# Two attention blocks and a feed-forward over 16 sequences: the feed-forward's first weights and first norm prepared inside the last attention phase

## The chip, the core and the metric

One core of one Trainium2 chip runs the whole kernel. The metric is the time of one execution on the device, in microseconds (us). Engines: TensorE (PE, with its weight loads as PEld), VectorE (DVE), ScalarE (ACT), GpSimd (POOL) and SyncE (SP), which issues all the DMAs.

## What is computed

16 sequences of 256 tokens and 512 channels go through a layer with quantised attention, a gated feed-forward and a last attention:

```python
h1 = _ln(x, ln1_g, ln1_b)
x = _attn(h1, h1, a1_wq, a1_wk, a1_wv, a1_wo, a1_bo, d_q1, d_k1, d_v1, d_w1) + x
h2 = _ln(x, ln2_g, ln2_b)
x = _attn(h2, context, a2_wq, a2_wk, a2_wv, a2_wo, a2_bo, d_q2, d_k2, d_v2, d_w2) + x
h3 = _ln(x, ln3_g, ln3_b)
hg = h3 @ ff_w1 + ff_b1
a, g = jnp.split(hg, 2, axis=-1)
x = a * jax.nn.gelu(g, approximate=False) @ ff_w2 + ff_b2 + x
```

Then comes `_L1_xattn_ref`: 8-head attention with queries from this x and keys and values from the context, both normed. `_attn` rounds q, k, v and the probabilities to 8 bits. All matrices are 512 wide; the feed-forward is 512 to 4096 to 512.

## The kernel before, in words

**Attention part (first block of engine programs).** The work is a row of 32 phases, each one attention of one sequence, in 8 slots (groups) of two heads. In slot g the engines do, for the phase at hand: PE the scores of two groups ahead (`pe_scores`, odd slots only, both groups at once) and the probabilities times values of an earlier pair (`pe_pv`); DVE the row maxima (`dve_max`) and the scaling of the probabilities (`dve_probs`); POOL two tiny products, `pool_bias` and `pool_dsum`; ACT the exponentials (`act_exp`, four per group); SP the DMA transpose of the probabilities from `pq` to `pT` (`turn_probs`), which waits for the probabilities and for the P·V that frees its buffer. Into the slots are laid "fills", the projections for neighbouring phases, by hand-written tables such as `P_Y_FILLS`: `("k2", 0)` is the first half of the keys of attention 2, `o1` and `o2` the output projections, `h2T` the turning of the normed x on PE. Fills write the two PSUM banks `PJ` in turn; `act_quantise` (or `dve_residual`) empties them. The context is cast into a high and a low part (`ctxT`) in slots set by `ctx_at`: ACT in slot `ctx_at - 1`, DVE in `ctx_at`, POOL in `ctx_at + 1` (`pool_long`, ahead of POOL's other work of the slot).

All engines run in order, so every wait holds back what stands behind it. The last two phases are P_Y (attention 1 of the last sequence, with the fills for its attention 2) and P_Z (that attention 2). Behind P_Z come a drain (`pe_drain`: P·V of groups 4 to 7), the last output projection `o2@15`, its residual and its store to `mid_dram`; then all engines meet at a barrier.

**Feed-forward part (second block).** It is done in two halves of the hidden width. Each half holds 8 chunks f of the weights (256 columns of `ff_w1`, 128 rows of `ff_w2`) and passes over all 16 sequences ("rounds" below, `pe_sequence_a` in the first half). For a sequence PE does 8 times `pe_up` (24 matmuls into bank AG of f mod 2) and, two chunks behind, `pe_down` (6 matmuls into Y); between them the chunk's gate (ACT), product and cast (DVE) and low part (POOL); then the projections k and v of the context for the last attention. In round 0 of the first half the weights are made on the way: SP loads a chunk in three DMAs into one of two staging buffers, ACT casts it to the high part (`act_weights_high`), DVE subtracts to get the low part (`dve_weights_low`), and PE waits for `w_low_done`. Before that round the block needs the first sequence back from `mid_dram`, its norm on DVE and POOL (`ln_stats`, `ln_rstd`, `ln_xhat`), its turning on PE and its high and low parts (`h3_parts`). SP's order there: sequence 0, chunk 0, context, two rows, chunk 1, two pieces of `w2` (the weights Wk, Wv), chunk 2, then a wait for `base_ready`, sequence 1, store of `h3T`, chunk 3, and so on. `base` is sequence plus bias, made by POOL (`pool_base`, line 1870) behind the first `pool_mid_low`.

## Time and profile before

| | us |
|---|---|
| median of 3 runs | 2743.24 |
| lowest and highest run | 2740.99 to 2746.74 |
| the profiled execution, its own time | 2741.51 |
| its span in the trace | 2739.7 |
| barrier at the end of the attention part | 1062.58 |
| first AG matmul of the feed-forward | 1075.17 |

The page lists 54077 instructions; PE is busy 2575.7 us (94%), DVE 1642.4 (60%), ACT 1420.1 (52%), POOL 678.6 (25%). In its 40 slices of 68.5 us the digits of PE are 9 nearly everywhere but for the first two slices and the 15th and 16th, 6 and 4 (959 to 1096 us), where the granted clock also stands at 7 tenths. Times in the trace are counted from the start of the span; a line such as `L701` is a line of the kernel before.

### The profile page before, as it was taken

The page shows a single profiled execution, that of the slowest core. Times are in us where ns is not written, and L with a number is a line of the kernel's source. Part 1 is how long each engine was busy: PE and PEld are TensorE (multiplying, and loading weights), DVE is VectorE, ACT ScalarE, POOL GpSimd, SP SyncE. Part 2 cuts the span into 40 slices and gives each one's busy share as a digit, 9 for nine tenths or more (in the row PEclk, how much of TensorE's full clock was granted, in tenths as well). Part 3 has the DMA queues.
Part 4 walks back from the last instruction along what each step waited for, and adds up shares of the span by engine and source line. Part 5 has one row for each costly group of instructions (what it writes and reads, how often), then busy time and mean ns, then how long its engine had stood idle before and what let it go on. Part 6 is the DMA issues. An engine that isn't in the chain of part 4 may idle for free.

```text
span 2739.7 us, 54077 instructions
## 1 busy us (share of the span) xinstructions
PE 2575.7 (94%) x18304; PEld 2151.3 (79%) x18304; DVE 1642.4 (60%) x3945; ACT 1420.1 (52%) x3749; POOL 678.6 (25%) x1147
## 2 busy tenths in 40 slices
PE   5799999999999964999999999999999999999997
PEld 4566676676667642899999999999888888888885
DVE  6799999999999964634444443454443444444444
ACT  5688888888888862211112111123555555555554
POOL 1222222222222211323222222322221222222211
PEclk9899999999999977999999999999999999999998
DMA  4444444444444535311121211141111111111111
GB/s 151 94 95 100 93 98 97 100 92 96 99 93 96 93 63 144 105 69 69 54 84 54 77 56 74 61 150 66 47 54 38 54 54 46 46 46 54 46 38 39
DMA packets 335273, 211.06 MB, mean 77 GB/s; under 512 B 275568, under 2 KB 291952, under 8 KB 335216
## 3 DMA queue, kind: packets, MB, share of 16 engines
q1 hardware_dynamic: 335216, 210.34, 28.8%
q8 instruction: 31, 0.51, 0.1%
q14 instruction: 26, 0.21, 0.0%
HBM read 92.84 MB, written 50.33 MB: 52 GB/s over the span
## 4 chain that ended last, share of the span: by engine, by line
PE 56%; DVE 2%; issue 1%; ACT 1%; DMA 0%; POOL 0%; DVEq 0%; SPq 0%; POOLq 0%
PE AG L156 35%; PE Y L156 13%; PE XT L1314 3%; PE O L1337 2%; PE XT L1324 2%; PE XT L131 1%; DVE parts L1658 1%; DVE xhat L123 1%; PE Y L131 1%; PE O L1347 0%; DVE turned L185 0%; ACT stage L1554 0%; DMA stage<-in_ff_w_dram 0%; DVE mid_parts L1715 0%; POOL base L1870 0%
## 5 line engine op out<-in xcount | busy, mean ns | idle before, releaser
L156 PE MATMUL AG<-h_parts,up 128*128 128x256 f32 x6144 | 778.6, 284 | 13.4 <-DVE down L1639 10.1
L156 PEld LDWEIGHTS AG<-h_parts,up 128*128 128x128 f32 x6144 | 762.6, 192 | 26.0 <-issue 10.9
L599 ACT ACTIVATE e<-S,bias,qk_scale 128x256 f32<-128x256 f32 x1024 | 562.9, 569 | 113.5 <-POOL bias L805 113.5
L1522 ACT ACTIVATE gate<-AG,cols_pack 128x256 f32<-128x256 f32 x256 | 121.6, 475 | 668.8 <-PE AG L156 668.3
L1885 POOL TENSOR_TENSOR mid_parts<-mid_act,mid_parts 128x256 fp32r<-128x256 f32 x256 | 199.9, 781 | 1078.9 <-DVE mid_parts L1715 1078.9
L156 PE MATMUL Y<-down,mid_parts 128*128 128x512 f32 x1536 | 403.6, 399 | 0.0
L1708 DVE SCALAR_TENSOR_TENSOR mid_act<-AG,cols_pack,gate 128x256 f32<-128x256 f32 x256 | 123.4, 482 | 422.9 <-ACT gate L1522 421.9
L701 DVE TENSOR_REDUCE negmax<-S 128x4 f32<-128x1024 f32 x256 | 302.5, 1218 | 60.5 <-PE S L499 60.5
L156 PEld LDWEIGHTS Y<-down,mid_parts 128*128 128x128 f32 x1536 | 271.9, 189 | 68.7 <-issue 22.6
L719 DVE TENSOR_SCALAR pq<-e,rsum 128x256 uint16<-128x256 f32 x1024 | 292.1, 348 | 15.7 <-DMA pT<-pq 3.0
L147 PE MATMUL PJ<-w_a_wo,oT 128*128 128x512 f32 x512 | 239.4, 612 | 3.6 <-ACT oT L608 2.7
L156 PE MATMUL PJ<-hT,w_a_wq 128*128 128x256 f32 x1536 | 205.9, 292 | 29.9 <-DVE hT L690 24.5
L156 PEld LDWEIGHTS PJ<-hT,w_a_wq 128*128 128x128 f32 x1536 | 193.7, 197 | 46.0 <-issue 29.5
L599 ACT ACTIVATION_READ_ACCUMULATOR e<-S,bias,qk_scale 128x1 f32 x1024 | 212.7, 208 | 0.0
L156 PEld LDWEIGHTS AG<-parts,w_late 128*128 128x128 f32 x1536 | 190.5, 191 | 4.5 <-issue 0.6
L156 PE MATMUL AG<-parts,w_late 128*128 128x256 f32 x1536 | 192.0, 283 | 0.0
L147 PEld LDWEIGHTS PJ<-w_a_wo,oT 128*128 128x128 f32 x512 | 95.1, 195 | 109.1 <-issue 109.1
L567 ACT ACTIVATE q<-PJ,inv 128x512 int8<-128x512 f32 x192 | 130.6, 701 | 91.1 <-PE PJ L156 91.1
L1744 DVE TENSOR_REDUCE negmax<-XT 128x2 f32<-128x512 f32 x128 | 82.5, 686 | 104.9 <-PE XT L1314 104.9
L1715 DVE CAST mid_parts<-mid_act 128x256 fp32r<-128x256 f32 x256 | 84.4, 330 | 86.5 <-PE Y L156 82.1
L1554 ACT ACTIVATE stage<-XT,negmax 128x256 f32<-128x256 f32 x256 | 118.1, 473 | 29.0 <-DVE negmax L1744 28.5
L1522 ACT ACT_TABLE_LOAD x59 | 75.7, 1283 | 109.4 <-PE AG L156 109.0
(125 smaller groups left out, 3411.4 us busy)
## 6 DMA issues: line engine op xcount, KB each, us to landing
stage<-in_ff_w_dram SPq DMA_DIRECT2D x48, 256.0 KB, 4.9
x_in<-in_x_dram SPq DMA_DIRECT2D x16, 512.0 KB, 3.9
...
```

What stands on the lines that cost most here:

```text
L147: last = nc.tensor.matmul(bank[:], xT[:, k, j * P:(j + 1) * P], w[:, k, :], start=(k == 0), stop=(k == KC - 1))
L156: last = nc.tensor.matmul(acc, lhs(l), rhs(r), start=(start and i == 0), stop=(stop and i == 2))
L567: nc.scalar.activation(q8[:, bank, :], PJ[bank][:], ACT.Copy, scale=inv[:, d:d + 1]).then_inc(pj_emptied[bank], 1)
L599: nc.scalar.activation(e[:, g % E_BUFS, i, :], S[g % 2][:, i // 2, i % 2, :], ACT.Exp, bias=bias[:, g % 2, i:i + 1], scale=qk_scale[:, ph. ...
L701: nc.vector.tensor_reduce(negmax[:, g % 2, :], S[g % 2][:].rearrange("p i q n -> p (i q) n"), AX_X, ALU.max, negate=True).then_inc(max_don ...
L719: nc.vector.tensor_scalar(pq[:, s, i, :].bitcast(U16), e[:, g % E_BUFS, i, :], rsum[:, s, i:i + 1], WMAX, ALU.mult, ALU.min).then_inc(prob ...
L1522: nc.scalar.activation(gate[:, f % 2, :], AG[f % 2][:, TOK:2 * TOK], ACT.Gelu, bias=ff_b1[:, c:c + 1]).then_inc(gate_done, 1)
L1554: nc.scalar.activation(e4[:, h % 2, qt, :], X4[h % 2][:, qt, :], ACT.Exp, bias=negmax4[:, h % 2, qt:qt + 1], accum_out=sums4[:, qt, h:h + ...
L1708: nc.vector.scalar_tensor_tensor(out=mid_act[:, f % 2, :], in0=AG[f % 2][:, 0:TOK], scalar=ff_b1[:, c:c + 1], in1=gate[:, f % 2, :], op0=A ...
L1715: nc.vector.tensor_copy(mid_parts[:, f % 2, 0, :], mid_act[:, f % 2, :]).then_inc(mid_high_done, 1)
L1744: nc.vector.tensor_reduce(negmax4[:, h % 2, :], X4[h % 2], AX_X, ALU.max, negate=True).then_inc(max4_done, 1)
L1885: nc.gpsimd.tensor_tensor(mid_parts[:, f % 2, 1, :], mid_act[:, f % 2, :], mid_parts[:, f % 2, 0, :], ALU.subtract).then_inc(mid_low_done, 1)
```

## The change

Buffers: `weights`, `stage`, `x_in`, `xhat`, `turned`, `hT` and the PSUM banks `PJ` now belong to both blocks. The six attention weights lie in the tile that later holds the feed-forward's chunks, and `ctx_in`, `x_bo` and the second q and k buffers lie in `stage`. The places of chunks 0 to 3 hold a1_wq, a1_wk and a1_wv, which are last read before P_Y.

Work moved from the start of the second block into P_Z: the load of sequence 0 and its norm, its turning (behind P_Z's last slot), its high and low parts; load, cast and subtraction of chunks 0 to 3. SP issues sequence 0 and chunks 0 and 1 behind the transpose of group 0, chunk 2 behind that of group 4, chunk 3 behind that of group 5. ACT and DVE do the chunks at the ends of slots 2, 3, 5 and 7.

Work reordered: in P_Y the k2 fills go from slot 4 to slots 2 and 3 and the casting of the context one slot ahead (`ctx_at` 1 for 2); in P_Z the second o2 fill goes from slot 3 to slot 5, the store of sequence 14 from behind group 4 to behind group 6, and `pool_x1_bo` of the last sequence behind the phase. In the second block round 0 starts at once; its chunks 4 to 7 are cast in f = 1 to 4, and the last two pieces of `w2` are loaded behind chunks 6 and 7.

```diff
@@ -78,6 +78,21 @@
+        weights = sb(ctx, "weights", [P, FC // 2, 3072], F32R)
+        weights_flat = weights[:].rearrange("p f n -> p (f n)")
+        stage = sb(ctx, "stage", [P, 3, 1024])
+        stage_up = stage[:, 0:2, :].rearrange("p s (g k n) -> p s g k n", g=2, k=KC)
+        stage_down = stage[:, 2, :].rearrange("p (s d) -> p s d", s=2)
+        up = weights[:, :, 0:2048].rearrange("p f (l k g n) -> p f l k g n", l=2, k=KC, g=2)
+        down = weights[:, :, 2048:3072].rearrange("p f (l d) -> p f l d", l=2)
+        x_in = sb(ctx, "x_in", [P, TT, D])
+        xhat = sb(ctx, "xhat", [P, TT, D])
+        turned = sb(ctx, "turned", [P, KC, TOK])
+        hT = sb(ctx, "hT", [P, 2, KC, TOK], F32R)
+        PJ = [ps(ctx, f"PJ{i}", [P, 512]) for i in range(2)]
@@ -215,8 +230,9 @@
                      5: both("h2T", "q2"), 6: [("v2", 0)], 7: both("hT") + [("v2", 1)]}
-        P_Y_FILLS = {3: both("o1"), 4: both("k2"), 5: both("h2T", "q2"), 6: [("v2", 0)], 7: [("v2", 1)]}
-        P_Z_FILLS = {3: both("o2")}
+        P_Y_FILLS = {2: [("k2", 0)], 3: [("k2", 1)] + both("o1"), 5: both("h2T", "q2"), 6: [("v2", 0)],
+                     7: [("v2", 1)]}
+        P_Z_FILLS = {3: [("o2", 0)], 5: [("o2", 1)]}
@@ -271,7 +287,7 @@
-                self.ctx_at = {id(PHASE2_FILLS): 4, id(P_A_FILLS): 4, id(P_Y_FILLS): 2}.get(id(fills))
+                self.ctx_at = {id(PHASE2_FILLS): 4, id(P_A_FILLS): 4, id(P_Y_FILLS): 1}.get(id(fills))
@@ -337,20 +353,18 @@
-            w1 = {n: sb(one, "w_" + n, [P, 2, KC, D], F32R) for n in WEIGHTS}
+            w1 = {n: weights_flat[:, i * 4096:(i + 1) * 4096].rearrange("p (l k d) -> p l k d", l=2, k=KC)
+                  for i, n in enumerate(WEIGHTS)}
-            x_in = sb(one, "x_in", [P, TT, D])
-            ctx_in = sb(one, "ctx_in", [P, KC, TOK])
-            x_bo = sb(one, "x_bo", [P, TT, D])
+            ctx_in = stage[:, 1].rearrange("p (k n) -> p k n", k=KC)
+            x_bo = stage[:, 0].rearrange("p (t d) -> p t d", t=TT)
-            xhat = sb(one, "xhat", [P, TT, D])
-            turned = sb(one, "turned", [P, KC, TOK])
-            hT = sb(one, "hT", [P, 2, KC, TOK], F32R)
-            qT = [sb(one, f"qT{i}", [P, KC, TOK], BF16) for i in range(2)]
-            kT = [sb(one, f"kT{i}", [P, KC, TOK], BF16) for i in range(2)]
+            second_qk = stage[:, 2].bitcast(BF16).rearrange("p (i k n) -> p i k n", i=2, k=KC)
+            qT = [sb(one, "qT0", [P, KC, TOK], BF16), second_qk[:, 0]]
+            kT = [sb(one, "kT0", [P, KC, TOK], BF16), second_qk[:, 1]]
@@ -658,8 +676,11 @@
                     if ph.ctx_at is not None and g == ph.ctx_at - 1:
                         act_ctx_high(act, ph, prev)
+                    if ph is P_Z and g in CHUNK_AT:
+                        act_ahead_chunk(act, CHUNK_AT[g])
 
             def act_drain(act, ph):
+                act_ahead_turned(act)
                 act_oT(act, ph, 1)
 
 
@@ -772,6 +793,13 @@
+                    if ph is P_Z and g in CHUNK_AT:
+                        dve_ahead_chunk(dve, CHUNK_AT[g])
+                    if ph is P_Z and g == 4:
+                        dve.wait_ge(early_sem["y_loaded"], 16)
+                        ln_stats(dve, early_sem["ln4"], x_in, 0)
+                    if ph is P_Z and g == 5:
+                        ln_xhat(dve, early_sem["ln4"], x_in, xhat, 0)
@@ -797,6 +825,7 @@
                 dve_probs(dve, ph, GROUPS - 1)
+                dve_ahead_turned(dve)
             def pool_bias(pool, ph, g):
@@ -854,8 +883,6 @@
-                    if ph is P_Z and g in (6, 7):
-                        pool_x1_bo(pool, ph.b, g - 6)
@@ -869,6 +896,8 @@
+                    if ph is P_Z and g == 4:
+                        ln_rstd(pool, early_sem["ln4"], 0)
@@ -876,6 +905,72 @@
+            AHEAD_CHUNKS = 4
+            CHUNK_AT = {2: 0, 3: 1, 5: 2, 7: 3}
+            def sp_ahead_sequence(sp):
+                sp.wait_ge(x_bo_done, B)
+                sp.wait_ge(x2_stored, 16 * (B - 2) + 1)
+                sp.dma_start(x_in[:], mid[0]).then_inc(early_sem["y_loaded"], 16)
+            def sp_ahead_chunk(sp, f):
+                if f == 0:
+                    for j in range(TT):
+                        wait_emptied(sp, ("last", B - 2, "o1", j))
+                    sp.wait_ge(ctx_low_done, 2 * B)
+                    sp.wait_ge(scores_done, P_Y.group(GROUPS))
+                if f >= 2:
+                    sp.wait_ge(early_sem["w_low_done"], 2 * (f - 1))
+                for g in range(2):
+                    sp.dma_start(stage_up[:, f % 2, g],
+                                 w_view(t["ff_w1"])[:, :, g * FF + f * P:g * FF + (f + 1) * P]).then_inc(
+                        early_sem["up_staged"][f % 2], 16)
+                sp.dma_start(stage_down[:, f % 2, :], t["ff_w2"][f * P:(f + 1) * P, :]).then_inc(
+                    early_sem["down_staged"][f % 2], 16)
+            def act_ahead_chunk(act, f):
+                act.wait_ge(early_sem["up_staged"][f % 2], 32 * (f // 2 + 1))
+                nc.scalar.copy(up[:, f, 0].rearrange("p k g n -> p g k n"), stage_up[:, f % 2]).then_inc(
+                    early_sem["w_high_done"], 1)
+                act.wait_ge(early_sem["down_staged"][f % 2], 16 * (f // 2 + 1))
+                nc.scalar.copy(down[:, f, 0, :], stage_down[:, f % 2, :]).then_inc(early_sem["w_high_done"], 1)
+            def dve_ahead_chunk(dve, f):
+                dve.wait_ge(early_sem["w_high_done"], 2 * (f + 1))
+                nc.vector.tensor_tensor(up[:, f, 1].rearrange("p k g n -> p g k n"), stage_up[:, f % 2],
+                                        up[:, f, 0].rearrange("p k g n -> p g k n"), ALU.subtract).then_inc(
+                    early_sem["w_low_done"], 1)
+                nc.vector.tensor_tensor(down[:, f, 1, :], stage_down[:, f % 2, :], down[:, f, 0, :],
+                                        ALU.subtract).then_inc(early_sem["w_low_done"], 1)
+            def pe_ahead_turn(pe):
+                for j in range(2):
+                    wait_emptied(pe, ("last", B - 1, "o2", 1 - j))
+                    pe.wait_ge(early_sem["ln4"]["xhat_done"], TT)
+                    transpose_chunks(PJ[j], xhat, j).then_inc(early_sem["xt_filled"][j], 1)
+            def act_ahead_turned(act):
+                act.wait_ge(early_sem["xt_filled"][0], 1)
+                affine_act(turned, PJ[0], 0, cols["ln3_g"], cols["ln3_b"], early_sem["xt_emptied"][0])
+                act.wait_ge(early_sem["xt_emptied"][0], 1)
+                nc.scalar.copy(hT[:, 0, 0:2, :], turned[:, 0:2, :]).then_inc(early_sem["h3_high_done"][0], 1)
+            def dve_ahead_turned(dve):
+                dve.wait_ge(early_sem["xt_filled"][1], 1)
+                affine_dve(turned, PJ[1], 1, cols["ln3_g"], cols["ln3_b"], early_sem["xt_emptied"][1])
+                dve.wait_ge(early_sem["xt_emptied"][1], 1)
+                nc.vector.tensor_copy(hT[:, 0, 2:4, :], turned[:, 2:4, :]).then_inc(early_sem["h3_high_done"][1], 1)
+                dve.wait_ge(early_sem["h3_high_done"][1], 1)
+                nc.vector.tensor_tensor(hT[:, 1, 2:4, :], turned[:, 2:4, :], hT[:, 0, 2:4, :],
+                                        ALU.subtract).then_inc(early_sem["h3_low_done"], 1)
+            def pool_ahead_low(pool):
+                pool.wait_ge(early_sem["h3_high_done"][0], 1)
+                nc.gpsimd.tensor_tensor(hT[:, 1, 0:2, :], turned[:, 0:2, :], hT[:, 0, 0:2, :],
+                                        ALU.subtract).then_inc(early_sem["h3_low_done"], 1)
@@ -971,7 +1066,10 @@
-                    turn_phase(P_Z, {4: [lambda: store("last", B - 2)]})
+                    turn_phase(P_Z, {
+                        0: [lambda: sp_ahead_sequence(sp), lambda: sp_ahead_chunk(sp, 0), lambda: sp_ahead_chunk(sp, 1)],
+                        4: [lambda: sp_ahead_chunk(sp, 2)], 5: [lambda: sp_ahead_chunk(sp, 3)],
+                        6: [lambda: store("last", B - 2)]})
@@ -1004,6 +1102,9 @@
                     pool_phase(pool, P_Z, None)
+                    for j in range(TT):
+                        pool_x1_bo(pool, B - 1, j)
+                    pool_ahead_low(pool)
@@ -1098,7 +1199,10 @@
                     pe_phase(pe, P_Z, P_Y, None)
+                    pe_ahead_turn(pe)
                     pe_drain(pe, P_Z)
+                    for j in range(2):
+                        pe.wait_ge(early_sem["xt_emptied"][j], 1)
                     for j in range(2):
                         pe_fill(pe, ("last", B - 2, "o2@15", j))
...
@@ -1785,7 +1884,7 @@
-                        if first(b) and f + READY < HC:
+                        if first(b) and f and f + READY < HC:
@@ -1924,7 +2023,7 @@
-                READY = HC - AHEAD_FROM if attends else 1
+                READY = HC - AHEAD_FROM if attends else AHEAD_CHUNKS - 1
@@ -2019,25 +2118,21 @@
                                     load_w2(1)
                             return
                         if not attends:
-                            load_y(0)
-                            load_chunk(0)
                             load_kv(0)
                             for i, n in enumerate(ROWS2):
                                 sp.dma_start(rows2[:, i], t[n].partition_broadcast(P)).then_inc(rows2_loaded, 16)
-                            load_chunk(1)
                             for i in range(2):
                                 load_w2(i)
-                            for f in range(2, HC):
+                            for f in range(AHEAD_CHUNKS, HC):
                                 load_chunk(f)
-                                if f == 2:
-                                    sp.wait_ge(ln4["xhat_done"], TT)
+                                if f == AHEAD_CHUNKS:
                                     sp.wait_ge(base_ready, 1)
                                     load_y(1)
                                     store_h3(0, 1)
-                                if f in (3, 4):
-                                    sp.wait_ge(w2_low_done, f - 2)
-                                    load_w2(f - 1)
+                                if f > HC - 3:
+                                    sp.wait_ge(w2_low_done, f - HC + 3)
+                                    load_w2(f - HC + 4)
                             sp.wait_ge(ln4["xhat_done"], TT * (turn_no(0, "cT") + 1))
                             load_kv(1)
                             store_h3(1, turn_no(0, "h3T'") + 1)
@@ -2111,12 +2204,6 @@
-                            dve.wait_ge(y_loaded, 16)
-                            ln_stats(dve, ln4, y_in, 0)
-                            ln_xhat(dve, ln4, y_in, xhat2, 0)
-                            dve_weights_low(dve, 0)
-                            dve_post_h3(dve, 0, "h3T")
-                            dve_h3_parts(dve, 0)
@@ -2148,8 +2232,6 @@
-                            for j in range(2):
-                                pe_turn(pe, 0, "h3T", j)
```

**Where instructions move.** POOL in P_Y, before: the context's low part stands behind the product `dsum` of group 2, with both `bias` products of the pair ahead of it.

```order
L826 TENSOR_TENSOR x<-x,rows 128x512 [waits x2_stored,prob_scaled]
L811 TENSOR_TENSOR dsum<-sums,delta_w 128x4 [waits exp_done]
L805 TENSOR_TENSOR bias<-negmax,qk_scale 128x4 [waits max_done] x2
L811 TENSOR_TENSOR dsum<-sums,delta_w 128x4 [waits exp_done]
L836 TENSOR_TENSOR ctxT<-ctx_in,ctxT 128x512 [waits ctx_high_done,prob_scaled]
```

The same place in the change (lines of the new file):

```order
L855 TENSOR_TENSOR x<-x,rows 128x512 [waits x2_stored,prob_scaled]
L840 TENSOR_TENSOR dsum<-sums,delta_w 128x4 [waits exp_done]
L834 TENSOR_TENSOR bias<-negmax,qk_scale 128x4 [waits max_done]
L865 TENSOR_TENSOR ctxT<-stage,ctxT 128x512 [waits ctx_high_done,prob_scaled]
L834 TENSOR_TENSOR bias<-negmax,qk_scale 128x4 [waits max_done]
```

The subtraction, which waits for the probabilities of group 1, now stands between the pair's two bias products.

SP in P_Z, in the change (the first row ends with the transpose of P_Z's group 0; `stage` rows are the chunks' loads; before, these rows were transposes and two stores of `x` alone):

```order
L1029 DMA_TRANSPOSE pT<-pq 128x8x128 [waits prob_scaled,pv_done] x10
L917 DMA x_in<-mid_dram 128x1024 [waits x2_stored,x_bo_done]
...
L1029 DMA_TRANSPOSE pT<-pq 128x8x128 [waits prob_scaled,pv_done] x4
L928 DMA stage<-in_ff_w_dram 128x4x128 [waits w_low_doneA]
L928 DMA stage<-in_ff_w_dram 128x4x128
L931 DMA stage<-in_ff_w_dram 128x512
L1029 DMA_TRANSPOSE pT<-pq 128x8x128 [waits prob_scaled,pv_done]
L928 DMA stage<-in_ff_w_dram 128x4x128 [waits w_low_doneA]
```

Chunk 2 stands between the transposes of groups 4 and 5, chunk 3 behind that of group 5.

DVE at the end of P_Z, in the change (`negmax` of groups 6 and 7, chunk 2, `xhat`, the probabilities of group 5, the residual, those of group 6, chunk 3, and then those of group 7):

```order
L722 TENSOR_REDUCE negmax<-S 128x4 [waits scores_done] x2
L943 TENSOR_TENSOR weights<-stage,weights 128x2x4x128 [waits w_high_doneA]
L946 TENSOR_TENSOR weights<-stage,weights 128x512
L138 TENSOR_SCALAR xhat<-x_in,mv,rstd 128x512 [waits lnA_rstd_done]
L138 TENSOR_SCALAR xhat<-x_in,mv,rstd 128x512
L730 RECIPROCAL rsum<-dsum 128x4 [waits dsum_done]
L740 TENSOR_SCALAR pq<-e,rsum 128x256 [waits probs_turned3,rsum_done]
...
L943 TENSOR_TENSOR weights<-stage,weights 128x2x4x128 [waits w_high_doneA]
L946 TENSOR_TENSOR weights<-stage,weights 128x512
L730 RECIPROCAL rsum<-dsum 128x4 [waits dsum_done]
```

Before, nothing stood between the maxima of groups 6 and 7 and the probabilities of groups 5, 6 and 7; now two rows of chunk 2 stand ahead of group 5's and two of chunk 3 ahead of group 7's.

## Rows read from the trace of the kernel before

**Rows 1.** The page, part 4: the chain that ended last, by engine.
```profile
PE 56%; DVE 2%; issue 1%; ACT 1%; DMA 0%; POOL 0%; DVEq 0%; SPq 0%; POOLq 0%
```
**Rows 2.** Windows: stretch, length, busy us per engine, granted clock, DMA share, GB/s.
```profile
965.00:1008.18 43.18, 29.59 (x182) 20.82 (x181) 25.58 (x65) 23.23 (x72) 7.65 (x19) 0.80 0.27 53
1008.18:1062.58 54.40, 26.30 (x132) 11.43 (x132) 24.71 (x59) 21.70 (x70) 6.06 (x19) 0.75 0.33 68
1062.58:1132.21 69.63, 48.55 (x313) 45.05 (x314) 44.56 (x79) 26.41 (x40) 18.93 (x20) 0.83 0.57 174
1132.21:1179.63 47.42, 47.23 (x329) 43.85 (x329) 20.05 (x51) 8.18 (x17) 13.51 (x16) 1.00 0.18 68
...
1070.00:1080.00 10.00, 6.74 (x30) 6.34 (x31) 6.73 (x8) 4.49 (x6) 1.26 (x1) 0.50 0.97 301
```
**Rows 3.** Chain of waits at the feed-forward's start: start, us, what.
```profile
1088.13 5.75 DMA stage<-in_ff_w_dram
...
1093.90 0.95 ACT up L1449
...
1095.50 0.98 DVE up L1636
...
1096.64 0.69 DVE down L1639
...
1132.21 14.07 PE AG L156 x96
```
**Rows 4.** PE's timeline in P_Y: start, us, instruction, idle before and releaser.
```profile
974.96 0.61 PE L499 MATMUL S<-kT,qT 32*128 32x256 bf16 x8 [5.65 <-ACT e L599]
...
977.04 9.31 PE L147 MATMUL PJ<-w_a_wo,oT 128*128 128x512 f32 x16 [0.91 <-ACT oT L608]
...
997.66 7.47 PE L156 MATMUL PJ<-hT,w_a_wq 128*128 128x256 f32 x48 [3.36 <-DVE hT L690]
```
**Rows 5.** DVE's and POOL's timeline in P_Y's slots 2 and 3.
```profile
971.47 1.13 DVE L719 TENSOR_SCALAR pq<-e,rsum 128x256 uint16<-128x256 f32 x4
...
975.01 1.26 POOL L836 TENSOR_TENSOR ctxT<-ctx_in,ctxT 128x512 fp32r<-128x512 f32 x1 [2.02 <-DVE pq L719]
```
**Rows 6.** PE's timeline in P_Z and its drain.
```profile
1008.18 0.40 PE L499 MATMUL S<-kT,qT 32*128 32x256 bf16 x8 [0.31 <-ACT e L599]
...
1021.37 0.61 PE L499 MATMUL S<-kT,qT 32*128 32x256 bf16 x8 [5.86 <-ACT e L599]
...
1023.44 10.00 PE L147 MATMUL PJ<-w_a_wo,oT 128*128 128x512 f32 x16 [0.91 <-ACT oT L608]
...
1048.60 0.62 PE L524 MATMUL O<-pT,vQ 128*32 128x256 f16 x8 [5.73 <-DMA pT<-pq]
...
1050.12 8.61 PE L147 MATMUL PJ<-w_a_wo,oT 128*128 128x512 f32 x16 [0.90 <-ACT oT L608]
```
**Rows 7.** SP's transpose of P_Z's group 0, and ACT's first chunk cast (timelines).
```profile
1015.61 2.12 SPq L934 DMA_TRANSPOSE pT<-pq  x1
...
1067.82 1.04 ACT L1449 CAST up<-stage 128x1024 fp32r<-128x1024 f32 x1 [17.85 <-DMA stage<-in_ff_w_dram]
```
**Rows 8.** DVE's timeline: probabilities of P_Z's groups 4 and 7.
```profile
1034.29 1.14 DVE L719 TENSOR_SCALAR pq<-e,rsum 128x256 uint16<-128x256 f32 x4
...
1044.14 1.14 DVE L719 TENSOR_SCALAR pq<-e,rsum 128x256 uint16<-128x256 f32 x4
```
**Rows 9.** A chunk loaded alone in the second half: SP's issue, ACT's cast.
```profile
1850.35 0.94 SPq L1962 DMA_DIRECT2D stage<-in_ff_w_dram  x2
...
1854.14 1.05 ACT L1449 CAST up<-stage 128x1024 fp32r<-128x1024 f32 x1
```
**Rows 10.** POOL's timeline: `base` of sequence 0 and of sequence 1; SP's load behind.
```profile
1082.77 3.94 POOL L1870 TENSOR_TENSOR base<-own,rows 128x512 f32<-128x512 f32 x2
...
1086.78 0.34 SPq L1940 DMA_DIRECT2D own<-mid_dram  x1
...
1142.65 2.55 POOL L1870 TENSOR_TENSOR base<-own,rows 128x512 f32<-128x512 f32 x2
```

51 lines of the change are left out of this document (22 added, 29 removed).

## The prediction

> **What bounds the kernel now.** I read the page's chain first: PE holds 56% of it and no other engine over 2% [rows 1], so over most of the span only less work for PE would help. The change takes none away; it aims at the one place where PE stands still, so I read windows next [rows 2]. A round of the feed-forward in steady state takes 47.42 us with PE busy 47.23 at full clock. The stretch from the barrier (1062.58) to the first v projection of round 0 (1132.21) takes 69.63 with PE busy 48.55 at a mean clock of 0.83. P_Y's stretch (965 to 1008.18) and P_Z with its drain (54.40 us) have PE busy 29.59 and 26.30 us at 0.80 and 0.75. So the last 97 us of attention aren't bound by PE: there scores, maxima, exponentials, probabilities and transposes follow each other, each releasing the next. That is where the change puts its new work.
>
> **Term 1, the feed-forward's start: a gain of 18.0 us.** The steady chain's piece of 96 matmuls is two v fills (24 matmuls 512 wide) and the first three "up" chunks (72, 256 wide): v is 48/120 of 14.07 us, 5.6 [rows 3]. A round at full speed therefore takes 47.4 - 5.6 = 41.8 us from its first "up" to its v. After the change PE can start at the barrier. What is left of delay, counted from the barrier:
> - Half clock at the start: PE has stood still about 4 us (its last matmuls end at 1058.7 [rows 6], the barrier is at 1062.58). The clock falls as it did there, the first 24-matmul chunks cost about 2 us more, and chunks 0 to 2 and "down" 0 end at +12.0.
> - "Up" 3 needs its bank emptied, which needs gate 1, and ACT does gate 1 behind the cast of chunk 4. Ahead of chunk 4 in the queue stand the context, two rows, two w2 pieces: 2.5 MiB with its own "up" part, 8.7 us at 301 GB/s [rows 2], plus 1.8 (sequence 0 and chunk 0 are 1 MiB, 3.5 us, and chunk 0 was ready 5.24 us after the first issue [rows 7]). That is +10.5; casts and subtractions of the chunk, 1093.90 to 1097.33, 3.4 [rows 3], the w2 piece and the gate's product 2.1: "up" 3 at +16, not +12. With a clock that falls again it and "down" 1 end at +22.6.
> - Chunk 5 stands behind `base_ready`. First "up" at half clock to +5.0, gate to low part +2.1, `base` 2.6: +9.7. From the load behind `base` to a cast chunk's start there are 7.1 us (1086.78 to 1093.90 [rows 10, 3]): +16.9. Casts, w2 piece, product and the norm of the context then end at +23.5, one us after PE wants it.
> - From there 27.5 us of PE's work and 0.6 of waiting for the second norm: v at +51.6.
>
> That is 69.6 - 51.6 = 18.0. Bounds: 50.0 (chunk 5 is 1.5 sooner) to 55.0 (chunk 4 and 5 both late, `base` slow). `base` took 3.94 us beside DVE's subtractions and 2.55 alone [rows 10]; DVE waits at that time in the change, so I take 2.6. The Trainium skill, "SBUF — State Buffer", section "Who interferes with whom", says that VectorE with two SBUF inputs and GpSimd reading SBUF lock each other out; the two rows agree, and if they met here after all the gain would be 16.6.
>
> **Term 2, P_Y: a loss of 4.6 us.** Moving k2 into an idle slot looks free, but its operand isn't ready. POOL's low part of the context waits for the probabilities of group 1. These ended at 972.6 [rows 5]; now they are later by 0.6 (ACT casts its context part between the two exponentials that release the next scores) and 1.06 (DVE's context work stands ahead of them): 974.3, and with 1.26 of POOL k2 can start at 975.7. The scores of groups 4 and 5, at 974.96 before [rows 4], stand behind it on PE. At half clock for some 4 us it takes 4.9 (2.9 full, 5.8 half): 980.6. Scores and P·V, second k2 fill (2.9): 984.1. Two o1 fills at full clock, 3.5 each: 991.2, where they ended at 986.35 before. The norm of x1, the turning and the q2 fills hang on that; k2 no longer stands between o1 and the turning, but that gap was filled by the norm as well. I take 4.6 for the start of P_Z's first scores (1008.18 before [rows 6]); ends 2.5 (clock full at once) and 6.
>
> **Term 3, P_Z and drain: a loss of 17.4 us.** Offsets are from P_Z's first scores.
> - The transpose of group 0 leaves SP at +7.4 to +9.6 [rows 7]. Then come sequence 0 and chunk 0, cast from +14.9 (the 5.24 us again), down part to +17.0. ACT does this ahead of the exponentials of group 3, which could begin at +10.8. They end at +19.2, and the scores of group 4, at +13.2 before [rows 6], start at +19.4: 6.2 late.
> - The o2 fill begins at +21.4 and takes 6.6 at half clock (two took 10.00 [rows 6]); residual 0.7, the new statistics 1.6, and with 1.3 for themselves the probabilities of group 4 end at +31.7. Before +27.25 (1035.43 [rows 8]): 4.5 late, since the second o2 fill no longer stands ahead of the scores of group 6.
> - Now the chain of loads. The transpose of group 4 takes SP 1.4; chunk 2 is ready 4.5 later (3.79 alone [rows 9], 5.75 in company [rows 3]; nearest to the lone one, with a transpose ahead); ACT 1.65 and DVE 1.9 (1093.90 to 1095.50 to 1097.33 with a little for the hand-over [rows 3]), `xhat` 1.0, probabilities of group 5 1.35; transpose 1.4, chunk 3 4.5, ACT 1.65, DVE 1.9, probabilities of group 7 1.35. Sum 22.6 us from the end of group 4's probabilities to the end of group 7's; before, 9.85 (1035.43 to 1045.28 [rows 8]). 12.8 late.
> - The rest is as before: last P·V 3.3 us later, barrier 13.98 behind it [rows 6].
>
> 4.5 + 12.8 = 17.3, and 0.1 for hand-overs: 17.4; ends 15.9 (3.8 us per load) and 20 (5.75).
> The Trainium skill, "DMA: Bandwidth & Descriptors", section "Anatomy of one DMA — SWDGE (gpsimd) path", puts a transfer at 2.0 us plus bytes over 436 GB/s: an estimate of 3.7 for a chunk's "up" part with its second issue, which would make term 3 smaller by 1.6. By it the sum would be +2.4. The section is written of another issuing path; here no load was under 3.79.
>
> **What costs nothing.** The four casts and subtractions for chunks 0 and 1 beyond the wait above stand beside other engines' chain; if not, 1.6 each. `pool_x1_bo` behind the phase waits for the store of sequence 14, about 7 us ahead of its reader. PE's turning and the h parts are done while the transpose of group 7 is under way. The shared buffers hold the same sizes; the loop of phases and rounds 1 to 15 issue what they did.
>
> **Sum.** -18.0 + 4.6 + 17.4 = +4.0 us. On the profiled execution's 2741.5 that is 2745.5; the median of the runs is 1.7 higher, so I say 2747.2. What a measurement can tell from no change is 0.2%, 5.5 us, so this is within it: the start of the feed-forward is bought with an equally long tail.
>
> **Rival 1, slower: the clock.** Longer waits in P_Y and P_Z leave PE at 1.2 GHz where I counted full clock. For it: both stretches stand at 0.75 to 0.80 already [rows 2], and the q2 fills took 7.47 us, 5.7 at full clock [rows 4]. Whole at half: k2 +0.9, q2 +2.5 beyond today's loss, o2 +0.6, first and fourth "up" of the feed-forward +1.5 together: +5.5, total +9.5, 2752.7. It decides as soon as 1.5 us are lost beyond my count. Against it: in each fill longer than 6 us the clock came back within it. Dearer loads (5.75 each, +2.5) lead to the same side. Chance of the side 0.37.
>
> **Rival 2, faster: P_Y isn't delayed.** k2's fill fills PE's idle 5.65 us [rows 4], keeps the clock up through the o1 fills (9.31 would be 7.0) and the scores start no later than today; P_Y then gives 2.3 instead of costing 4.6, and with loads of 3.8 us the total is -4.3 - 1.4, 2737.5. Against it stand the order of POOL and the waits of [rows 5]. Chance 0.15.
>
> **How the numbers follow.** The forecast and its neighbourhood within 0.2% have 0.48, rival 1's side 0.37, rival 2's 0.15; these are the chances of same, slower and faster. The bounds of the terms, taken together as if one or two were at an end at a time, reach from -7 to +12 us about the median; the range is 2736 to 2755.
>
> **What would show it.** After: the barrier about 22 us later, at 1084.5 (1080 to 1089), and the first AG matmul within 0.3 us of it. Barrier to the first v 51.6 us. POOL's context row in P_Y starting on the probabilities at about 974.4, P_Z's first scores at 1012.8. In ACT's waits, two or more for the loads of chunks 0, 2 and 3, 3 to 8 us each, and DVE's subtractions waiting behind. Between the probabilities of groups 4 and 7 some 22.6 us. I am wrong if the barrier moves by less than 12 us (the chunk chain overlaps) or the first v comes later than 56 us behind it.

## The result, and the profile after

| | before | changed |
|---|---|---|
| median, us (13 runs each, one chip) | 2742.21 | 2748.98 |
| ratio of the two, 95% interval | | 1.0026, 1.0018 to 1.0033 |
| second comparison, other chip (15 and 11 runs) | 2743.39 | 2749.30, 1.0020 (1.0011 to 1.0029) |
| the profiled execution, own time and span | 2741.51, 2739.7 | 2748.55, 2746.8 |

The change makes the kernel slower by 0.2 to 0.26%, 6 to 7 us, where +4.0 was forecast. The time lies in the range; both intervals exclude no change, and both hold the 0.2% that separates "same" from "slower" in the prediction. One execution of py_before (6381.09 us) and one of casts_behind (3632.38 us), two of the experiments below, were slow; they stand outside the ratios, not outside the medians.

Below, "7.14 for 9.31" means 7.14 us where it was 9.31 us (or where that was expected), and a time with a plus is counted from P_Z's first scores or, at the feed-forward's start, from the barrier.

First the windows of the changed kernel, cut as those of before [rows 2]: P_Y's stretch (from 965.00 in both), P_Z with its drain, the feed-forward's start to the first v, one steady round. One cut of before differs: PE's row of the first v begins at 1132.05, 0.16 us ahead of the 1132.21 of [rows 2 and 3], and the changed kernel is cut at that row.

```profile
965.00:1012.78 47.78, 29.83 (x183) 22.00 (x181) 25.52 (x65) 23.39 (x72) 8.31 (x19) 0.79 0.23 49
1012.78:1086.60 73.82, 29.10 (x140) 12.84 (x140) 37.97 (x78) 29.05 (x81) 8.77 (x22) 0.66 0.41 100
1086.60:1139.05 52.45, 46.43 (x305) 43.45 (x305) 28.85 (x60) 18.82 (x29) 16.70 (x17) 0.89 0.51 161
1139.05:1186.47 47.42, 47.23 (x329) 43.85 (x328) 20.04 (x51) 8.18 (x17) 13.49 (x16) 1.00 0.18 68
```

```profile
1132.05 5.60 PE L156 MATMUL AG<-w_late,parts 128*128 128x512 f32 x24
```
```profile
1139.05 5.60 PE L171 MATMUL AG<-w_late,parts 128*128 128x512 f32 x24
```

P_Y is 4.60 us longer, P_Z 19.42 longer, the start of the feed-forward 17.02 shorter (52.45 for 69.47, both to the rows above); the round behind takes 47.42 us in both. The first v comes 7.00 us later, nearly the whole difference of the two executions (7.04). PE's busy time hardly moved (P_Z 29.10 for 26.30, 1.97 of it the turning that came from the other block). What moved is idle time, out of the feed-forward and into P_Z.

P_Y, on POOL and PE (start, us, instruction, idle before and releaser):

```profile
974.33 1.26 POOL L865 TENSOR_TENSOR ctxT<-stage,ctxT 128x512 fp32r<-128x512 f32 x1 [3.44 <-DVE pq L740]
```
```profile
975.73 4.50 PE L171 MATMUL PJ<-ctxT,weights 128*128 128x256 f32 x24 [5.84 <-POOL ctxT L865]
980.17 0.40 PE L517 MATMUL S<-stage 32*128 32x256 bf16 x8
...
983.80 7.14 PE L162 MATMUL PJ<-w_a_wo,oT 128*128 128x512 f32 x16
...
1012.78 0.40 PE L517 MATMUL S<-kT,qT 32*128 32x256 bf16 x8 [0.31 <-ACT e L617]
```

k2's first fill stands in PE's queue ahead of the scores of groups 4 and 5, and waits 5.84 us for POOL's low part. The scores start at 980.17 for 974.96 [rows 4]. The o1 fills keep full clock (7.14 for 9.31) but end at 990.9 for 986.35.

P_Z, on ACT, DVE, POOL and PE:

```profile
1027.52 1.04 ACT L936 CAST weights<-stage 128x1024 fp32r<-128x1024 f32 x1 [3.89 <-DMA stage<-in_ff_w_dram]
...
1047.93 1.04 ACT L936 CAST weights<-stage 128x1024 fp32r<-128x1024 f32 x1 [8.74 <-DMA stage<-in_ff_w_dram]
...
1059.46 1.04 ACT L936 CAST weights<-stage 128x1024 fp32r<-128x1024 f32 x1 [5.02 <-DMA stage<-in_ff_w_dram]
```
```profile
1041.17 1.14 DVE L740 TENSOR_SCALAR pq<-e,rsum 128x256 uint16<-128x256 f32 x4
...
1049.52 1.23 DVE L943 TENSOR_TENSOR weights<-stage,weights 128x1024 fp32r<-128x1024 f32 x1 [4.96 <-ACT weights L939]
...
1061.06 1.23 DVE L943 TENSOR_TENSOR weights<-stage,weights 128x1024 fp32r<-128x1024 f32 x1 [5.68 <-ACT weights L939]
...
1063.01 3.95 DVE L740 TENSOR_SCALAR pq<-e,rsum 128x256 uint16<-128x256 f32 x4
```
```profile
1062.37 2.90 POOL L855 TENSOR_TENSOR x<-x,rows 128x512 f32<-128x512 f32 x2 [8.23 <-DMA mid_dram<-x]
1065.23 1.31 POOL L972 TENSOR_TENSOR hT<-turned,hT 128x512 fp32r<-128x512 f32 x1
```
```profile
1031.42 0.62 PE L517 MATMUL S<-kT,qT 32*128 32x256 bf16 x8 [11.19 <-ACT e L617]
...
1033.49 5.37 PE L162 MATMUL PJ<-w_a_wo,oT 128*128 128x512 f32 x8 [0.91 <-ACT oT L626]
...
1070.31 0.62 PE L542 MATMUL O<-pT,vQ 128*32 128x256 f16 x8 [12.82 <-DMA pT<-pq]
1071.83 10.10 PE L162 MATMUL PJ<-w_a_wo,oT 128*128 128x512 f32 x16 [0.91 <-ACT oT L626]
```

These are the three load waits on ACT that term 3 names, with DVE's subtraction behind each. The scores of group 4 stand behind the first, the probabilities of groups 5 and 7 behind the other two. The probabilities of group 4 end at 1042.31, those of group 7 at 1066.96: 24.65 us, 9.85 before [rows 8]. One row isn't in the prediction at all: the four scalings of group 7 took 3.95 us, those of group 4 1.14. POOL's two additions, and its part of the turned norm behind them, run beside the slow ones only.

The feed-forward's start, on PE and ACT:

```profile
1086.79 10.94 PE L171 MATMUL AG<-hT,weights 128*128 128x256 f32 x72 [4.86 <-PEq L979]
...
1103.90 5.20 PE L171 MATMUL AG<-hT,weights 128*128 128x256 f32 x24 [4.78 <-DVE spacer L1816]
```
```profile
1098.55 1.04 ACT L1548 CAST weights<-stage 128x1024 fp32r<-128x1024 f32 x1 [6.05 <-DMA stage<-in_ff_w_dram]
...
1103.95 1.05 ACT L1548 CAST weights<-stage 128x1024 fp32r<-128x1024 f32 x1 [2.52 <-DMA stage<-in_ff_w_dram]
```

PE starts 0.19 us behind the barrier (12.59 before) and has one more long wait before the first v, 4.78 us ahead of "up" 3, for the gate that ACT does behind chunk 4's load.

### The profile page after: what moved, and what is told of

It is laid out like the page before. It is cut to its first block, busy times and chain, and to the rows that moved or that the text cites. A ratio compares the mean times of both kernels' runs of the same rounds, so it can differ in the third digit from the quotient of the medians.

```text
span 2746.8 us, 54080 instructions
## 1 busy us (share of the span) xinstructions
PE 2578.2 (94%) x18304; PEld 2153.7 (78%) x18304; DVE 1638.9 (60%) x3945; ACT 1418.4 (52%) x3749; POOL 678.6 (25%) x1147
## 4 chain that ended last, share of the span: by engine, by line
PE 56%; DVE 2%; issue 1%; DMA 0%; ACT 0%; POOL 0%; DVEq 0%; SPq 0%; POOLq 0%; ACTq 0%
PE AG L171 35%; PE Y L171 12%; PE PJ L1413 3%; PE O L1436 2%; PE PJ L1423 2%; PE PJ L146 1%; DVE parts L1757 1%; DVE xhat L138 1%; PE Y L146 1%; PE O L1446 0%; DVE turned L200 0%; DMA rows<-in_bv_dram 0%; DMA stage<-in_ff_w_dram 0%; ACT stage L1653 0%; DVE mid_parts L1814 0%
## 5 line engine op out<-in xcount | busy, mean ns | idle before, releaser
L171 PE MATMUL AG<-hT,weights 128*128 128x256 f32 x6144 | 778.7, 285 | 9.7 <-PEq L979 4.9
L171 PEld LDWEIGHTS AG<-hT,weights 128*128 128x128 f32 x6144 | 762.9, 193 | 22.2 <-issue 5.7
L171 PE MATMUL Y<-weights,mid_parts 128*128 128x512 f32 x1536 | 403.6, 399 | 0.0
L171 PE MATMUL PJ<-hT,weights 128*128 128x256 f32 x2304 | 303.2, 291 | 30.0 <-DVE hT L711 24.4
L171 PEld LDWEIGHTS PJ<-hT,weights 128*128 128x128 f32 x2304 | 288.1, 196 | 49.5 <-issue 29.6
L171 PEld LDWEIGHTS Y<-weights,mid_parts 128*128 128x128 f32 x1536 | 271.9, 189 | 68.7 <-issue 22.6
L1843 DVE TENSOR_REDUCE negmax<-PJ 128x2 f32<-128x512 f32 x128 | 82.4, 686 | 104.7 <-PE PJ L1413 104.7
L840 POOL TENSOR_TENSOR dsum<-sums,delta_w 128x4 f32<-128x4 f32 x256 | 69.9, 273 | 260.2 <-ACT e L617 260.2
```

What stands on the lines that cost most here:

```text
L171: last = nc.tensor.matmul(acc, lhs(l), rhs(r), start=(start and i == 0), stop=(stop and i == 2))
L1843: nc.vector.tensor_reduce(negmax4[:, h % 2, :], X4[h % 2], AX_X, ALU.max, negate=True).then_inc(max4_done, 1)
```

## The experiments

Ten variants, and the changed kernel once more. The ratio is to before, on the same chip. The medians come from several chips, on which before took 2742.21 to 2743.94 us, so kernels of different chips are compared by their ratios. "P_Z" runs from its first scores to the barrier, "start" from the barrier to PE's row of the first v, both from the profiled execution. The absolute start of P_Z isn't compared between kernels: with the same order in P_Y it lay anywhere from 1008.18 to 1012.79 us. For before and changed it can be: the scores ahead of P_Y come at 954.52 and 954.59. P_Y is read as the stretch from the last scores of the phase ahead of it to P_Z's first.

| kernel | median | ratio (95%) | P_Z | start |
|---|---|---|---|---|
| before | 2742.21 | 1 | 54.40 | 69.47 |
| changed | 2748.98 | 1.0026 (1.0018 to 1.0033) | 73.82 | 52.45 |
| changed, repeated | 2749.30 | 1.0020 (1.0011 to 1.0029) | 73.83 | 52.20 |
| py_before | 2745.73 | 1.0006 (0.9996 to 1.0015) | 74.87 | 51.81 |
| x1bo_held | 2747.90 | 1.0012 (1.0003 to 1.0021) | 69.87 | 52.54 |
| loads_early | 2736.81 | 0.9975 (0.9966 to 0.9985) | 60.36 | 53.19 |
| casts_behind | 2746.60 | 1.0010 (1.0002 to 1.0019) | 70.02 | 52.72 |
| z_order_only | 2740.52 | 0.9987 (0.9978 to 0.9996) | 50.26 | 69.69 |
| all_moved | 2725.65 | 0.9939 (0.9926 to 0.9953) | 54.03 | 52.26 |
| z_all | 2730.31 | 0.9953 (0.9939 to 0.9966) | 53.79 | 52.64 |
| two_ahead | 2727.17 | 0.9938 (0.9925 to 0.9950) | 55.00 | 55.07 |
| gate_first | 2724.79 | 0.9930 (0.9917 to 0.9943) | 53.98 | 53.99 |
| norm_first | 2728.70 | 0.9944 (0.9931 to 0.9958) | 54.10 | 55.03 |

**py_before: P_Y's order taken back.**

```diff
-        P_Y_FILLS = {2: [("k2", 0)], 3: [("k2", 1)] + both("o1"), 5: both("h2T", "q2"), ...
+        P_Y_FILLS = {3: both("o1"), 4: both("k2"), 5: both("h2T", "q2"), ...
...
-                               ... id(P_Y_FILLS): 1}
+                               ... id(P_Y_FILLS): 2}
```

> The changed kernel with one part taken back: the phase ahead of the last has the projection k2 in slot 4 and the context's split one slot later again, as before. Theory (the three terms add, and nothing in the last phase waits for a point of time outside it): the last phase's first scores come back from 1012.78 to about 1008.2 us, and the time is 4.6 us less than the changed kernel's, about 2744.4. Rival (the delay of that phase is taken up later, where the last phase waits for its loads anyway): first scores at 1008.2, but the barrier within 1.5 us of 1086.6, and a gain of 0 to 1.5.

The ratio falls by 0.0020 against the first comparison of the changed kernel and by 0.0014 against the second, 5.5 and 3.8 us. P_Y's stretch is 52.74 us:

```profile
957.18:1009.92 52.74, 38.94 (x245) 26.95 (x245) 34.83 (x84) 29.85 (x93) 9.15 (x25) 0.87 0.33 61
```

In the changed kernel it is 58.19 (954.59 to 1012.78). Over all profiles, seven with the old order have 52.7 to 54.6 (mean 53.8), six with the new one 58.1 to 59.9 (mean 58.4): 4.6 us. The rival wants P_Z longer by what P_Y is shorter, and the time down by at most 1.5 us; P_Z was 1.05 longer, and the time fell by more. The rival falls. The theory's absolute times did not come (first scores at 1009.92, not 1008.2).

**x1bo_held: POOL's additions behind the last probabilities.**

```diff
+                    pool.wait_ge(prob_scaled, 4 * P_Z.group(GROUPS))
                     for j in range(TT):
                         pool_x1_bo(pool, B - 1, j)
                     pool_ahead_low(pool)
```

> The changed kernel, with POOL's two additions of x1 and a2_bo and the turned norm's low half held back until the last probabilities are made. Theory (the four scalings of group 7 on DVE took 3.95 instead of 1.14 us because POOL's 512-wide additions ran beside them): they take 1.14 us again, transpose(7) issues 2.8 us sooner, the time is 2.8 us less than the changed kernel's, about 2746.2. Rival (ScalarE's cast of chunk 3 and its turning of the norm, or the DMA transfers, slow DVE there): the scalings still take over 3 us and the time is the same within 0.5 us. A second rival: the additions move beside DVE's turned norm and slow that, and half of the 2.8 us comes back.

DVE and POOL at the place of the 3.95 us:

```profile
1062.45 1.14 DVE L740 TENSOR_SCALAR pq<-e,rsum 128x256 uint16<-128x256 f32 x4
1063.51 0.99 DVE L200 TENSOR_SCALAR turned<-PJ,cols_pack 128x256 f32<-128x256 f32 x2
1064.54 0.68 DVE L965 CAST hT<-turned 128x512 fp32r<-128x512 f32 x1
1065.25 1.63 DVE L967 TENSOR_TENSOR hT<-turned,hT 128x512 fp32r<-128x512 f32 x1
```
```profile
1063.67 2.66 POOL L855 TENSOR_TENSOR x<-x,rows 128x512 f32<-128x512 f32 x2 [9.97 <-DVE pq L740]
```

The scalings take 1.14 again while ACT still casts and turns as in the changed kernel, so it was POOL's work. The additions and the part of the turned norm moved together, so the two aren't told apart. From P_Z's first scores to the last P·V 54.73 us are left of 57.53: 2.80. P_Z as a whole is 3.95 shorter; the other 1.15 is behind the last P·V, 0.32 in the o2 fills (9.78 for 10.10) and 0.8 in the store's landing (3.03 for 3.85 us from its issue to the barrier). The second rival is there, and harmless: now the subtraction of the turned norm takes 1.63 instead of 0.69, beside an idle PE. The whole time fell by 0.0014 and 0.0008 of before, 2 to 4 us.

**loads_early: the chunk loads one slot sooner.**

```diff
-                        4: [lambda: sp_ahead_chunk(sp, 2)], 5: [lambda: sp_ahead_chunk(sp, 3)],
+                        3: [lambda: sp_ahead_chunk(sp, 2)], 4: [lambda: sp_ahead_chunk(sp, 3)],
```

> The changed kernel, with SP's issues of chunks 2 and 3 one slot sooner: behind transpose(3) and transpose(4) instead of transpose(4) and transpose(5); the casts stay where they are. Theory (the last phase is long because ACT stands at the head of its queue for transfers that were issued 4.2 to 4.5 us before): the idle 8.74 us ahead of the cast of chunk 2 and the 5.02 us ahead of that of chunk 3 shrink to under 3 us each, the barrier comes 7 to 11 us sooner, the time is about 2739.5. Rival (the loads only follow a chain that is long for its own work, the casts, subtractions and xhat): a gain of at most 3 us. Rival (the loads then collide with the transposes and land later): 0 to 4 us.

The same casts on ACT:

```profile
1044.23 1.04 ACT L936 CAST weights<-stage 128x1024 fp32r<-128x1024 f32 x1 [4.13 <-DMA stage<-in_ff_w_dram]
...
1050.65 1.07 ACT L936 CAST weights<-stage 128x1024 fp32r<-128x1024 f32 x1
```

P_Z is 13.5 us shorter, more than the 7 to 11 expected. 2.8 of it is the slow scaling, which took 1.14 here because POOL's additions came only at 1056.15, behind it; the loads alone are worth about 10.7, at the top of the span. One wait of 4.13 is left where under 3 was expected. The kernel is faster than before (0.9975, 0.9966 to 0.9985), 12 to 14 us less than the changed kernel by the ratios: two numbers in a table of slots turn the change's sign.

**casts_behind: chunks 0 and 1 a slot later.**

```diff
-            CHUNK_AT = {2: 0, 3: 1, 5: 2, 7: 3}
+            CHUNK_AT = {3: 0, 4: 1, 5: 2, 7: 3}
```

> The changed kernel, with the casts and subtractions of chunks 0 and 1 one slot later, behind the exponentials of groups 3 and 4, nothing else. Theory (term 3 has two parts, the wait for chunk 0's load ahead of exp(3), and the two loads behind probs(4)): the scores of group 4 come at +13.2 from the phase's first instead of +18.6, the probabilities of group 4 end 2 to 4 us sooner than +29.5, and the time is 2 to 4 us less than the changed kernel's, about 2746. Rival (the scores come sooner, but then wait for the output projection's first half and its clock at half, so that nothing is left of it): within 1 us of the changed kernel.

The scores of group 4 come at +13.18 (1028.80 from 1015.62), the probabilities of group 4 end at +26.8, 2.7 sooner; P_Z is 3.8 shorter, and by the ratios the time fell by 2.7 to 4.4 us, as the theory has it. The chain of loads behind is untouched: 24.8 us from there to the end of group 7's probabilities (24.65 in the changed kernel), with the slow scaling of 3.95 in it.

**z_order_only: the kernel before with the last phase's order alone.**

```diff
-        P_Z_FILLS = {3: both("o2")}
+        P_Z_FILLS = {3: [("o2", 0)], 5: [("o2", 1)]}
...
-                    if ph is P_Z and g in (6, 7):
-                        pool_x1_bo(pool, ph.b, g - 6)
...
-                    turn_phase(P_Z, {4: [lambda: store("last", B - 2)]})
+                    turn_phase(P_Z, {6: [lambda: store("last", B - 2)]})
...
+                    pool.wait_ge(prob_scaled, 4 * P_Z.group(GROUPS))
+                    for j in range(TT):
+                        pool_x1_bo(pool, B - 1, j)
```

> The kernel before, with the last phase's order alone: the second half of its output projection in slot 5 instead of slot 3, the store behind transpose(6), POOL's additions of x1 and a2_bo behind the last probabilities; nothing is made ahead. Theory (the reordering gives something by itself, since the last scores no longer stand behind the whole projection, and the changed kernel spends it): the probabilities of group 4 end 3.4 us sooner, the scaling of group 6 takes 1.14 instead of 1.90 us, and the time is 3.4 to 4.2 us less than before, about 2739. Rival (what the scores gain, the projection's second half and the later store take back ahead of the barrier): the same as before within 1 us.

P_Z 50.26 for 54.40. The probabilities of group 4 end at +23.7 (1034.36 from 1010.62) for +27.25, the scaling of group 6 takes 1.14. The reordering with POOL's additions held is worth 4.1 us of P_Z by itself, and 3.6 us of time (0.9987, 0.9978 to 0.9996). The changed kernel has the order, though not the hold (POOL waits for the store alone), and spends what it gains.

**all_moved: all of it together, and chunks 2 and 3 in the drain.** P_Y as before, POOL's additions held, loads one slot sooner, and:

```diff
-            CHUNK_AT = {2: 0, 3: 1, 5: 2, 7: 3}
+            CHUNK_AT = {3: 0, 4: 1}
...
                 act_ahead_turned(act)
+                act_ahead_chunk(act, 2)
                 act_oT(act, ph, 1)
+                act_ahead_chunk(act, 3)
...
                 dve_ahead_turned(dve)
+                dve_ahead_chunk(dve, 2)
+                dve_ahead_chunk(dve, 3)
```

> Everything that the three theories name, in one kernel: the phase ahead of the last as before; SP's issues of chunks 2 and 3 one slot sooner; casts and subtractions of chunks 0 and 1 behind the exponentials of groups 3 and 4 instead of ahead of them (slots 3 and 4), those of chunks 2 and 3 behind the last exponentials and probabilities; POOL's additions held back. Theory: the last phase and its tail cost 0 to 3 us more than before the change instead of 19.4, the feed-forward's start keeps its gain of 17.2, so the time is 2725 to 2729 us, faster than both. Rival (the four chunks' 6.6 us of ACT and 7.6 us of DVE lie on the path wherever they are put): 2732 to 2736. Rival (the feed-forward's start was short only because it had all four chunks long before the barrier; now chunks 2 and 3 are made late and round 0 waits): the barrier at about 1064, but the first v more than 55 us behind it.

Windows: P_Z, then the start of the feed-forward.

```profile
1009.88:1063.91 54.03, 28.84 (x140) 12.85 (x140) 38.33 (x78) 28.85 (x81) 10.14 (x22) 0.75 0.56 136
1063.91:1116.17 52.26, 45.85 (x304) 42.87 (x305) 28.85 (x60) 18.76 (x29) 15.75 (x17) 0.90 0.52 162
```

P_Z does the same work as in the changed kernel (DVE 38.33 busy for 37.97, ACT 28.85 for 29.05) in the time of before (54.03 for 54.40), and the start keeps its gain. 2725.65 us, 0.61% faster than before (0.47 to 0.74%). Both rivals fall: most of the chunk work never needed to be on the path.

Not all of it left the path. Beside z_order_only, which has the same order and nothing made ahead, P_Z is 3.8 us longer (54.03 for 50.26). DVE in all_moved, ahead of the probabilities of group 4:

```profile
1032.30 1.21 DVE L946 TENSOR_TENSOR weights<-stage,weights 128x1024 fp32r<-128x1024 f32 x1
1033.43 0.68 DVE L949 TENSOR_TENSOR weights<-stage,weights 128x512 fp32r<-128x512 f32 x1
1034.03 1.28 DVE L121 BATCH_NORM_STATS2 bn<-x_in 128x6 f32<-128x512 f32 x2
...
1035.69 1.14 DVE L741 TENSOR_SCALAR pq<-e,rsum 128x256 uint16<-128x256 f32 x4
```

The same scalings in z_order_only:

```profile
1033.22 1.14 DVE L719 TENSOR_SCALAR pq<-e,rsum 128x256 uint16<-128x256 f32 x4
```

They end at +26.95 for +23.74 from P_Z's first scores, 3.2 us later, and the subtraction of chunk 1 and the statistics of sequence 0 that stand ahead of them take about that. No run moved these two further.

**z_all: all_moved with P_Y's new order.**

```diff
-        P_Y_FILLS = {3: both("o1"), 4: both("k2"), 5: both("h2T", "q2"), ...
+        P_Y_FILLS = {2: [("k2", 0)], 3: [("k2", 1)] + both("o1"), 5: both("h2T", "q2"), ...
```

> all_moved, but with the phase ahead of the last in the changed kernel's order (k2 in slots 2 and 3 ahead of o1). Theory (term 2 stands by itself and adds): 4.6 us more than all_moved, about 2730.3. Rival (it only showed as 4.6 us because the last phase was bound otherwise): within 2 us of all_moved.

2730.31, 4.66 above all_moved in the medians. The two were measured on different chips; by the ratios it is 0.0014, 3.8 us, and the intervals overlap. The profiles are clearer: P_Y's stretch is 59.90 us for 54.59, P_Z and start together 106.43 for 106.29. P_Y's loss adds to a P_Z that is now short too.

**two_ahead: all_moved with two chunks instead of four.**

```diff
-            AHEAD_CHUNKS = 4
+            AHEAD_CHUNKS = 2
```

> all_moved, with two weight chunks made ahead instead of four; chunks 2 and 3 are loaded, cast and split in the feed-forward as the chunks behind them are. Theory (the first norm and the first two chunks take away the 12.6 us in which PE had nothing, and chunks 2 and 3 then only bring forward a row of loads that has a pace of its own): the first v 4 to 7 us later behind the barrier than the 52.3 us of all_moved, the time about 2731. Rival (with two chunks PE is covered until the loads come, and four are no better): within 1.5 us of all_moved. Rival (each chunk that is not ahead costs a whole load of 4 to 6 us): 2736 to 2738.

Start 55.07 for 52.26: 2.8 us, less than expected. In the time nothing is left to tell (0.9938 for 0.9939), though P_Z and start together are 3.8 longer in the profiles; but the profiled execution of two_ahead, 2732.07 us, was the slowest of its five, by 3.7 us. The first rival (four are no better than two) isn't ruled out. The second pair of chunks, on which the changed kernel spends its two long waits, brings 0 to 4 us.

**gate_first and norm_first: after the wait ahead of "up" 3.** gate(1) and its product ahead of chunk 4's cast and subtraction; then also gate(2) and the norm of the context ahead of chunk 5's. The diff is gate_first's on ACT; DVE's is alike.

```diff
                     for f in range(HC):
+                        if first(b) and f == 1:
+                            act_gate(act, b, f)
                         if first(b) and f and f + READY < HC:
                             act_weights_high(act, f + READY)
...
-                        act_gate(act, b, f)
+                        if not (first(b) and f == 1):
+                            act_gate(act, b, f)
```

> all_moved, and in the first feed-forward sequence gate(1) and its multiplication stand ahead of chunk 4's cast and subtraction on ACT and DVE instead of behind them. There PE stands still for 4.87 us behind up(2), because gate(1) waits in ACT's queue behind a cast whose load lands 11.4 us after the barrier. Theory (that stall is the order's, not the load's): the stall shrinks to under 1 us, up(4) finds chunk 4 ready, and the time is 3 to 5 us less than all_moved's, about 2721.6. Rival (the loads set the pace of the whole start, chunk 5 and the second pair of the K and V weights behind it): up(3) comes sooner but up(5) or the first k doesn't, and the time is that of all_moved within 1 us.

> gate_first again, with gate(2), its multiplication and the context's norm ahead of chunk 5's cast and subtraction too. In gate_first PE stood still 8.09 us behind up(3), ahead of the turning of the context's norm, which DVE had behind chunk 5. Theory (each stall at the start of the feed-forward is one of order, and goes when the item that PE waits for next stands ahead of the item that waits for a load): the 8.09 us shrink to under 4 us, the first v comes 48 to 50 us behind the barrier (52.26 in all_moved, 53.99 in gate_first), the time is about 2721. Rival (from here on the loads set the pace): the wait appears again ahead of up(5) to up(7) for chunks 5 to 7, the first v 52 to 54 us behind the barrier, the time 2724 to 2726.

"Up" 3 follows without a wait in both (1076.50 in gate_first, +11.8 instead of +16.8). But the idle time comes back: in gate_first 8.09 us ahead of the context's turning, in norm_first 4.11 there and 3.61 ahead of the turning of the next sequence:

```profile
1087.21 1.94 PE L146 MATMUL PJ<-ident,xhat 128*128 128x128 f32 x8 [4.11 <-DVE xhat L138]
...
1102.56 1.94 PE L146 MATMUL PJ<-ident,xhat 128*128 128x128 f32 x8 [3.61 <-DVE xhat L138]
```

The starts are 53.99 and 55.03 us, longer than all_moved's 52.26. The waits that were aimed at shrank or went, but both theories fall with the time they forecast; each wait taken away at the head comes back behind another norm. The rivals are right that nothing is won, and only in part about why: PE waits for norms that DVE makes behind the chunks, not for chunks 5 to 7 themselves. The chunks' loads are still in it, since ACT waited 3.37 us for chunk 5's in gate_first and 5.47 us for chunk 7's in norm_first; how much of PE's idle time is theirs isn't separated. In time neither can be told from all_moved (0.9930 and 0.9944 for 0.9939).

**after_again: the changed kernel, repeated.**

> The changed kernel as it is, on the chip of this comparison. Theory: 2748 to 2750 us, a ratio of 1.002 to 1.003 to before; the scaling of group 7 beside POOL's additions takes 3.5 to 4.0 us as before, since both start from fixed waits (the store's landing, and DVE's subtraction of chunk 3). Rival (the two met by chance in one execution): 1.14 us here.

1.0020, and the scalings of group 7 again take 3.95 us (1065.22, with POOL's additions at 1064.85). P_Z is 73.83 us, as in the first profile (73.82), but it is made up in another way: the probabilities of group 4 end at +31.6 for +29.5, from there to the end of group 7's it takes 24.3 us for 24.65, and the rest 17.95 for 19.64.

## Why the prediction was right, and where it was not

- **What bounds.** Right: only the 97 us of attention ahead of the barrier and the start behind it changed; they make 7.00 of the 7.04 us between the two executions.
- **Term 2, 4.6 us: right in size and, within 0.5 us, in each step.** POOL's row was due at 974.3 and came at 974.33, k2 at 975.7 and 975.73, the second fill's end at 984.1 and 983.8, P_Z's first scores at 1012.8 and 1012.78. py_before takes it away alone and z_all adds it alone (4.6 us in the mean of the profiles).
- **Term 3, 17.4 us: right in kind, 19.4 in size.** Three errors, of both signs, in the first profile. The step "the probabilities of group 4 end at +31.7" came 2.2 us too late (+29.5): chunk 0 was cast at +14.7 for +14.9, the scores came at +18.64 for +19.4, and the o2 half took 5.37 for 6.6. The chain of loads, 22.6 us, took 24.65. Its loads were right (4.19 and 4.50 us from issue to cast, 4.5 in the sum); the step that failed is "probabilities of group 7 1.35", which took 3.95; the other steps of the chain together were 0.8 shorter than summed. "The rest is as before" cost 2.3: o2's last fills 1.5 longer (10.10 for 8.61), and a store that landed 0.8 later (3.85 us from issue to barrier for 3.03). In the repeated profile only one of the three stands: the first step came at +31.6, as forecast, the rest cost 0.65 more than before, and the slow scaling of 3.95 was there again. So the scaling is what the prediction missed; the other two are within what one kernel does from one execution to the next.
- **Term 1, 18.0 us: 17.0.** 0.16 of it is the reading of before, where the first v begins at 1132.05 and not at 1132.21. "Up" 3 at +17.3 for +16, since chunk 4's cast started at +11.95 for +10.5; `base` done at +10.1 for +9.7, chunk 5's cast at +17.35 for +16.9, v at +52.45 for +51.6. Chunk 4's load is the step that was too short, by 1.45.
- **The sum.** Term 3 cost 2.0 more, term 1 gave 1.0 less: +7.0 for +4.0 between the profiled executions (+6.8 between the medians). The steps of term 3 missed in both directions, by up to 2.8 us; that its total still came within 2 us is in part luck.
- **"What costs nothing."** One place was wrong: `pool_x1_bo` was weighed by when its result is needed (7 us ahead), not by what runs beside it. For chunks 0 and 1 it holds in the changed kernel. In all_moved nearly everything of the four chunks fits beside the chain, but chunk 1's subtraction and the statistics put about 3.2 us on it.
- **Rival 1, the clock.** It exists in part: P_Z stands at 0.66 for 0.75, o2's last fills lose 1.5 us (0.6 in the repeat), the q2 fills 0.45 (7.92 for 7.47). That is 1 to 2 of the 5.5 us that it put beyond the count. Its side begins at +5.5, and the medians lie 6.8 apart: about one microsecond inside it, brought there as much by the slow scaling (2.8 us) as by the clock.
- **Rival 2** fell: k2 did keep the clock up for the o1 fills (7.14 us), and it was delayed all the same.
- **What the prediction didn't ask** is whether term 3 hangs on the work or on its place. It priced each load on the path nearly right, and never priced the same load issued a slot sooner.
